# Attention over sorted edges: the softmax weights move to a PSUM bank, and TensorE does the following pair's sums ahead of each step of the chain of maxima

## The chip, the cores and the metric

The kernel runs on one core of one Trainium2 chip. The time is that of one execution on the device in microseconds; the median of several runs counts. The profile is of one execution of its own.

## The reference, cut to what matters

A graph of 6250 nodes and 100,000 edges, sorted by `dst`, goes through two layers. The change is in the first one, an attention along the edges with 8 heads of 32 columns:

```
h = maximum(layernorm(x), 0)
q, k, v = h@Wq+bq, h@Wk+bk, h@Wv+bv          # (6250, 8, 32)
scores = einsum('ehd,ehd->eh', q[src], k[dst]) / sqrt(32)
m = segment_max(scores, dst)
e = exp(scores - m[dst]);  z = segment_sum(e, dst);  p = e / maximum(z[dst], 1e-16)
x = x + segment_sum(v[src] * p[:, :, None], dst)
```

The second layer (a hyperbolic message layer over the same edges) and the last node stage are untouched.

## The kernel before, in words

The kernel has five stages, one after the other: sorting the edges together with the projections, `attention`, `mid_stage`, `messages`, `fin_stage`. The change is inside `attention`.

**Units of work.** 128 edges lie on the 128 partitions and are one step. Two steps are a pair, whose edges all fall into one block of 127 nodes. A turn is 4 pairs (G = 8 steps, SG = 4), a window is 2 turns (16 steps x 8 heads = 128 columns). There are 440 pairs, 110 turns and 55 windows. The code is unrolled over 10 turns and looped.

**One turn `t`,** spread over the engines, each of which has its instructions in a fixed order of its own and waits on semaphores that count:

- SyncE fetches `marks` (which node each edge belongs to), penalties and columns.
- GpSimd issues 8 indirect gathers, one a step, of the rows q|v of `src` into one of 5 ring slots (L1935). A slot is free when VectorE has weighted the rows of the turn five before (`weighed`).
- ScalarE makes the one-hot matrices: `hot_columns` (L2033, L2035) for the products with k, `hot_rows` (L2045, L2048) for the sums.
- TensorE `near` (L1961, tile `kx`): one-hot times the block of k, a pair at a time. VectorE `mult` (L2126) multiplies by q, `score` (L2137) sums over 32 columns into `sc`.
- Three turns later VectorE `weigh` (L2105, two instructions a turn) multiplies the gathered v rows by the softmax weights `pw`, giving `pv`; ScalarE `weight_sums` (L2067) copies the weights beside them.
- Four turns later TensorE `sums` (L1981, tile `out`, two banks in turn) adds the rows of a pair by one-hot matrix, and VectorE `add` (L2147) adds the result into the block's accumulator. So `old` is turn t-4 and `ready` is turn t-3.

**The chain of maxima** runs once a window, in the even turns, and gives each edge the running maximum of its node. It goes back and forth between the two engines, one step for each p = 0..3 of the turn:

- TensorE p = 0: transpose of `sc` into `pT` (L1993, `t1_in`); it waits for `scored`. VectorE `runs_alone` (L2156, L2157, L2159) gives `ended`.
- TensorE p = 1: a small product (L1998, `m1_in`). VectorE `carries` (L2170, L2171) gives `carried`.
- TensorE p = 2: a small product (L2002, `m2_in`). VectorE `maxima` (L2180 to L2194) gives `cleared` and `readied`.
- TensorE p = 3: transpose of `shifted` into `ps` and a small product (L2006, L2008). ScalarE `weights` (L2056) takes exp from `ps` into `pw`, then exp of the block's factor into `fac` (L2059), which VectorE `rescale` (L2115) uses.

VectorE's order in slot p of a turn is `mult`, (`rescale`), `add`, `weigh` (p = 0, 1) or `score` (p = 2, 3), and then its step of the chain (p = 0, 1, 2). TensorE's is

```
sums(old, p)
near(t if p < 2 else t.plus(1), (p + 2) % SG)
if w:
    chain(t, w, p)
```

Of the kernel before, what the change touches and what calls it, by code (L numbers as in the profile page):

```python
# [11 lines left out]
ALU = mybir.AluOpType  # L12
ACT = mybir.ActivationFunctionType
AX = mybir.AxisListType

P = 128
NODES, DIM, HEADS = 6250, 256, 8
DH = DIM // HEADS
# [20 lines left out]
SCORE = 1.0 / math.sqrt(DH)  # L39
G = 8  # L40
# [24 lines left out]
class Stage(ExitStack):  # L65
# [6 lines left out]
    def sem(self, name):  # L72
        handle = self.enter_context(self.nc.semaphore(f"{self.tag}_{name}"))
        self.sems.append(handle)
        return handle
# [1675 lines left out]
SG = G // SPAN  # L1751
WSTEPS = P // HEADS
WG = WSTEPS // G
# [4 lines left out]
BODY = RING * WG  # L1758
# [55 lines left out]
def attention(nc, m, edges):  # L1814
# [17 lines left out]
    with Stage(nc, "at") as ctx:  # L1832
        sb = lambda n, s, d=F32: ctx.enter_context(nc.sbuf_tensor(f"at_{n}", s, d))
        pb = lambda n, s: ctx.enter_context(nc.psum_tensor(f"at_{n}", s, F32))
        sem = ctx.sem
# [7 lines left out]
        hot = sb("hot", [P, 2, G, P])  # L1843
        pv = sb("pv", [P, 2, G, HEADS, HD])
        sc = sb("sc", [P, WSTEPS, HEADS])
        pw = sb("pw", [P, BODY // WG, WSTEPS, HEADS])
        pens = sb("pens", [P, BODY // WG, PEN])
        off = sb("off", [1, SUPER], I16)
        blk = sb("blk", [P, 1 + SUPER])
# [9 lines left out]
        junk = sb("junk", [P, 2, WSTEPS])  # L1859
        kx = pb("kx", [P, 4, 512])  # L1860
        out = pb("out", [P, 2, 512])
        pT = pb("pT", [P, 512])
        ps = pb("ps", [P, 512])
        bc_in = [sem(f"bc_in{h}") for h in range(2)]
        col_in = m.at_col_in
        pen_in = [sem(f"pen_in{h}") for h in range(BODY // WG)]
        got = m.at_got
        (c_in, made, hotT_in, hot_in, z_in, kx_in, mixed, scored, weighed, out_in, summed, t1_in, ran, ended, m1_in, carried, m2_in,
         came_in, topped, cleared, readied, taken, t2_in, m3_in, far_rows, far_cols, p_in, fac_in, rescaled) = (sem(n) for n in (
             "c_in", "made", "hotT_in", "hot_in", "z_in", "kx_in", "mixed", "scored", "weighed", "out_in", "summed", "t1_in", "ran",  # L1870
             "ended", "m1_in", "carried", "m2_in", "came_in", "topped", "cleared", "readied", "taken", "t2_in", "m3_in", "far_rows",
             "far_cols", "p_in", "fac_in", "rescaled"))

        def window_of(t):

# [6 lines left out]
        with nc.Block() as block:  # L1882
# [57 lines left out]
            @block.tensor  # L1940
            def _(pe):
                TE = nc.tensor
                pe.wait_ge(c_in, 32)
                pe.wait_ge(made, 7)
                starts = Starts(pe, "at_pe", off, (NB - 1) * AW, 2)

                def near(t, p):


                    if not t.exists():  # L1950
                        return
                    if p % 2 == 0:
                        starts.fetch(t.n * SG + p, 2)
                    at = starts.values(p % 2, 1)[0]
                    if p == 0:
                        pe.wait_ge(hotT_in, t.n + 1)
                    before = t.plus(-1)
                    if before.exists():
                        pe.wait_ge(mixed, before.n * SG + p + 1)
                    for k in range(SPAN):  # L1960
                        last = TE.matmul(kx[:, p, k * DIM:(k + 1) * DIM], hotT[:, t.h % 2, (SPAN * p + k) * P:(SPAN * p + k + 1) * P],  # L1961
                                         m.keys[:, bass.ds(at, DIM)], start=True, stop=True)
                    last.then_inc(kx_in, 1)

                def sums(t, p):


                    if not t.exists():
                        return
                    if p == 0:  # L1970
                        pe.wait_ge(hot_in, t.n + 1)
                        pe.wait_ge(z_in, t.n + 1)
                    if p % 2 == 0:
                        pe.wait_ge(weighed, 2 * t.n + p // 2 + 1)
                    if p >= 2:
                        pe.wait_ge(summed, t.n * SG + p - 1)
                    elif t.plus(-1).exists():
                        pe.wait_ge(summed, t.plus(-1).n * SG + p + 3)
                    for k in range(SPAN):
                        j = SPAN * p + k  # L1980
                        last = TE.matmul(out[:, p % 2, 0:AW], hot[:, t.h % 2, j, :], pv[:, t.h % 2, j].rearrange("p h d -> p (h d)"),  # L1981
                                         start=(k == 0), stop=(k == SPAN - 1))
                    last.then_inc(out_in, 1)

                def chain(t, w, p):


                    n = w.window
                    if p == 0:
                        pe.wait_ge(scored, 2 * t.n)  # L1990
                        if w.plus(-WG).exists():
                            pe.wait_ge(cleared, n)
                        TE.transpose(pT[:, 0:P], sc.rearrange("p k h -> p (k h)"), m.ident[:, :]).then_inc(t1_in, 1)  # L1993
                    if p == 1:
                        pe.wait_ge(ended, n + 1)
                        if w.plus(-WG).exists():
                            pe.wait_ge(fac_in, n)
                        TE.matmul(ps[0:HEADS, 0:2 * WSTEPS], sel[:, :], ends.rearrange("p v k -> p (v k)"), start=True, stop=True).then_inc(m1_in, 1)  # L1998
                    if p == 2:
                        pe.wait_ge(carried, 2 * n + 2)  # L2000
                        both = carry[:, 0:2 * (WSTEPS + 2)].rearrange("h (v k) -> h v k", v=2)[:, :, 0:WSTEPS]
                        TE.matmul(ps[:, 4 * WSTEPS:6 * WSTEPS].rearrange("p (v k) -> p v k", v=2), selT.rearrange("h k g -> h (k g)"), both,  # L2002
                                  start=True, stop=True).then_inc(m2_in, 1)
                    if p == 3:
                        pe.wait_ge(cleared, n + 1)
                        TE.transpose(ps[:, P:2 * P], shifted[:, :], m.ident[:, :]).then_inc(t2_in, 1)  # L2006
                        pe.wait_ge(readied, 3 * n + 3)
                        TE.matmul(ps[:, 2 * P:2 * P + HEADS], first[:, :], scale[:, :], start=True, stop=True).then_inc(m3_in, 1)  # L2008

                def period(t):  # L2010
                    w = window_of(t)
                    old = t.plus(-LAG - 1)
                    for p in range(SG):
                        sums(old, p)
                        near(t if p < 2 else t.plus(1), (p + 2) % SG)
                        if w:
                            chain(t, w, p)

                near(Turn(0, 0), 0)
                near(Turn(0, 0), 1)  # L2020
                each_turn(pe, period, LAG + 1)

            @block.scalar
            def _(act):
# [25 lines left out]
                def weights(w):  # L2050
                    n = w.window
                    act.wait_ge(m3_in, n + 1)
                    act.wait_ge(t2_in, n + 1)
                    if w.plus(-BODY).exists():
                        act.wait_ge(weighed, 2 * (w.plus(-BODY).n + WG))
                    A.activation(pw[:, w.wslot].rearrange("p k h -> p (k h)"), ps[:, P:2 * P], ACT.Exp, scale=SCORE).then_inc(p_in, 1)  # L2056
                    if w.plus(-WG).exists():
                        act.wait_ge(summed, w.plus(-WG).n * SG + 1)
                    A.activation(fac[:, :], ps[:, 2 * P:2 * P + HEADS], ACT.Exp, scale=SCORE).then_inc(fac_in, 1)  # L2059

                def weight_sums(t):

                    if not t.exists():
                        return
                    act.wait_ge(p_in, t.window + 1)
                    k0 = (t.h % WG) * G
                    A.copy(pv[:, t.h % 2, :, :, DH], pw[:, t.wslot, k0:k0 + G, :]).then_inc(z_in, 1)  # L2067

                def period(t):
                    hot_columns(t.plus(1))  # L2070
# [10 lines left out]
            def _(dve):  # L2081
# [14 lines left out]
                def weigh(t, half):  # L2096
                    if not t.exists():
                        return
                    if half == 0:
                        dve.wait_ge(p_in, t.window + 1)  # L2100
                        if t.plus(-2).exists():
                            dve.wait_ge(out_in, t.plus(-2).n * SG + SG)
                    k = slice(half * (G // 2), (half + 1) * (G // 2))
                    k0 = (t.h % WG) * G + half * (G // 2)
                    V.tensor_tensor(pv[:, t.h % 2, k, :, 0:DH], ring[t.slot][:, k, DIM:2 * DIM].rearrange("p k (h d) -> p k h d", d=DH),  # L2105
                                    pw[:, t.wslot, k0:k0 + G // 2, :].unsqueeze(3).to_broadcast([P, G // 2, HEADS, DH]), ALU.mult).then_inc(weighed, 1)

                def rescale(t, at):

# [689 lines left out]
```

## Time and profile before

| | |
|---|---|
| median of 3 runs | 4433.48 us (4430.65 to 4446.2) |
| the profiled execution, its own time | 4412.6 us |
| its span, first to last instruction | 4410.7 us |
| VectorE busy | 3427.8 us (78%) |
| TensorE busy | 3227.8 us (73%) |
| ScalarE busy | 2222.8 us (50%) |
| GpSimd busy | 1967.7 us (45%) |
| attention stage | from about 742 to 2309 us |

The shares are means over five stages with different limits. The change touches the stage from 742 to 2309 us alone, so that stretch is to be read by itself. A wait that the profile calls `remote` ended with a semaphore update that has no recorded end of an instruction near it; `issue` is a wait that no update explains.

### The profile page before, as it was taken

Reading aid. Unit: us, or ns where it says so; the run is one execution under the profiler, and the core shown is the slowest. Engines: PE = TensorE matmul, PEld = TensorE weight load, DVE = VectorE, ACT = ScalarE, POOL = GpSimd, SP = SyncE. Lnnn points to the kernel's source line nnn. Section 1 sums busy time; section 2 is a strip of 40 time slices with the busy share of each in tenths; the row PEclk is TensorE's granted clock in tenths of the full one; section 3 lists DMA queues with packets and bytes.
Section 4 is the critical chain, followed back from the end, with each engine's and each line's share of the span. In section 5 each row is a group of like instructions: output and inputs, shape, how many; then the busy total and the mean of one; then the engine's idle time right before and its main releaser. Section 6 shows DMA issues by size and latency. Waiting matters only on the chain. (4 is left out here: it accounts for less than half of the span.)

```text
span 4410.7 us, 62580 instructions
## 1 busy us (share of the span) xinstructions
PE 3227.8 (73%) x12662; PEld 2489.5 (56%) x12663; DVE 3427.8 (78%) x9144; ACT 2222.8 (50%) x5988; POOL 1967.7 (45%) x2404
## 2 busy tenths in 40 slices
PE   3656653667767667776674688888888888988786
PEld 2434432545545555555553577777777777777654
DVE  8999995777767777777776377888888887888866
ACT  3245542434434444443446465665665665666556
POOL 1000003556555565555530266666666666666300
PEclk9767665788878888887887899999999999999987
DMA  2111005556666566666636465556555555555351
GB/s 61 36 52 36 20 17 168 172 177 198 187 180 193 179 198 192 188 194 179 194 121 166 139 172 165 157 159 164 157 158 164 161 158 162 162 159 158 89 119 47
DMA packets 295233, 635.08 MB, mean 144 GB/s; under 512 B 78196, under 2 KB 147122, under 8 KB 294656
## 3 DMA queue, kind: packets, MB, share of 16 engines
q0 software_dynamic: 141312, 463.96, 36.9%
q1 hardware_dynamic: 153602, 168.11, 13.7%
q14 instruction: 271, 2.22, 0.2%
q8 instruction: 48, 0.79, 0.1%
HBM read 587.26 MB, written 44.65 MB: 143 GB/s over the span
## 5 line engine op out<-in xcount | busy, mean ns | idle before, releaser
L2372 POOL DMA_INDIRECT area<-d_xr,col x880 | 904.0, 1027 | 733.9 <-DVE area L2609 305.9
L1935 POOL DMA_INDIRECT low<-d_qv,col x516 | 520.3, 1008 | 437.3 <-DVE at_pv L2105 270.8
L2465 PE MATMUL ms_near_a<-low,ms_hotT 128*128 x1760 | 564.7, 404 | 131.8 <-DVE area L2578 83.9
L1981 PE MATMUL at_out<-at_pv,at_hot 128*128 128x264 f32 x1760 | 582.1, 462 | 51.5 <-DVE area L2147 26.6
L1961 PE MATMUL at_kx<-area,tab_c 128*128 x1760 | 537.3, 436 | 31.5 <-issue 25.8
L2466 PE MATMUL ms_near_c<-tab_c,ms_hotT 128*128 x1760 | 554.6, 398 | 0.0
L2465 PEld LDWEIGHTS ms_near_a<-low,ms_hotT 128*128 128x128 f32 x1760 | 342.9, 199 | 215.0 <-issue 164.4
L1935 POOL DMA_INDIRECT tab_c<-d_qv,col x352 | 354.6, 1007 | 231.9 <-DVE at_pv L2105 118.4
L1961 PEld LDWEIGHTS at_kx<-area,tab_c 128*128 128x128 f32 x1760 | 385.9, 223 | 122.9 <-issue 49.0
L1981 PEld LDWEIGHTS at_out<-at_pv,at_hot 128*128 128x128 f32 x1760 | 368.1, 223 | 137.1 <-issue 57.5
L2485 PE MATMUL ms_out<-ms_more,ms_hot 128*128 128x257 f32 x1408 | 381.9, 395 | 74.9 <-DVE ms_hot L2599 63.8
L2507 ACT COPY area<-area 128x2 f32<-128x2 f32 x440 | 82.3, 187 | 632.1 <-DVE area L2578 516.5
L2147 DVE SCALAR_TENSOR_TENSOR area<-area,at_keep,at_out 128x264 f32 x440 | 212.2, 482 | 224.5 <-remote 132.2
L2466 PEld LDWEIGHTS ms_near_c<-tab_c,ms_hotT 128*128 128x128 f32 x1760 | 354.3, 201 | 57.1
L2575 DVE TENSOR_TENSOR ms_more<-area,ms_near_a 128x514 f32<-128x514 f32 x352 | 239.8, 681 | 174.7 <-PE ms_near_c L2468 114.9
L2056 ACT ACTIVATE at_pw<-at_ps 128x128 f32<-128x128 f32 x55 | 15.3, 278 | 669.4 <-PE at_ps L2008 349.5
L2485 PEld LDWEIGHTS ms_out<-ms_more,ms_hot 128*128 128x128 f32 x1408 | 269.5, 195 | 139.7 <-DVE low L2620 43.6
L2609 DVE CUSTOM_DVE_ANT_0 area<-area 128x256 f32<-128x256 f32 x880 | 337.0, 419 | 5.3 <-ACT area L2520 5.3
L2532 ACT ACTIVATE ms_junk<-ms_more 128x255 bf16<-128x255 f32 x704 | 282.2, 402 | 9.9 <-DVE ms_more L2575 0.8
L2599 DVE TENSOR_SCALAR ms_hot<-ramp,col,area 128x128 f32<-128x128 f32 x880 | 265.8, 349 | 11.8 <-issue 10.3
L2468 PE MATMUL ms_near_c<-area,ident 128*128 128x256 f32 x880 | 272.2, 392 | 0.0
L2045 ACT ACTIVATE at_hot<-ramp,col 128x128 f32<-128x128 f32 x880 | 267.5, 386 | 7.0 <-PE at_out L1981 5.2
(360 smaller groups left out, 6677.6 us busy)
## 6 DMA issues: line engine op xcount, KB each, us to landing
tab_c<-by_dst_marks SPq DMA_DIRECT2D x110, 512.0 KB
ms_near_no<-by_src_near SPq DMA_DIRECT2D x110, 224.0 KB
area<-d_xr,col POOLq DMA_INDIRECT x880
d_qv<-low SPq DMA_DIRECT2D x10, 1120.0 KB, 5.0
low<-d_qv,col POOLq DMA_INDIRECT x528
d_xr<-mid_hm SPq DMA_DIRECT2D x5, 1128.8 KB, 5.6
tab_c<-d_qv,col POOLq DMA_INDIRECT x352
first_x<-in_x_dram SPq DMA_DIRECT2D x5, 1120.0 KB
```

What stands on the lines that cost most here:

```text
L1935: pool.indirect_dma_start(out=ring[t.slot][:, k, :], out_offset=None, in_=m.d_qv, in_offset=bass.IndirectOffsetOnAxis(ap=col[:, t.h, k, 0: ...
L1961: last = TE.matmul(kx[:, p, k * DIM:(k + 1) * DIM], hotT[:, t.h % 2, (SPAN * p + k) * P:(SPAN * p + k + 1) * P], m.keys[:, bass.ds(at, DIM ...
L1981: last = TE.matmul(out[:, p % 2, 0:AW], hot[:, t.h % 2, j, :], pv[:, t.h % 2, j].rearrange("p h d -> p (h d)"), start=(k == 0), stop=(k == ...
L2045: A.activation(hot[:, t.h % 2, k, :], m.ramp[:, :], ACT.Abs, scale=-1.0, bias=col[:, t.h, k, 1:2].bitcast(F32)).then_inc(far_rows, 1)
L2372: pool.indirect_dma_start(out=far_rows(t, p)[:, k, :], out_offset=None, in_=m.d_xr, in_offset=bass.IndirectOffsetOnAxis(ap=col[:, t.h, SPA ...
L2465: TE.matmul(near_a[:, (SPAN * p + k) % 4, 0:TW], rows, m.tab_a[:, bass.ds(at, TW)], start=True, stop=True)
L2466: last = TE.matmul(near_c[:, p % 2, k * DIM:(k + 1) * DIM], rows, m.tab_c[:, bass.ds(at, DIM)], start=True, stop=p % 2 == 0)
L2468: last = TE.matmul(near_c[:, p % 2, k * DIM:(k + 1) * DIM], m.ident[:, :], far_rows(t, p)[:, k, XB:XW], start=False, stop=True)
L2485: last = TE.matmul(out[:, p % 2, 0:TW], hot[:, j, :], dd[t.slot][:, j, 0:TW], start=(k == 0), stop=(k == SPAN - 1))
L2532: AC.activation(junk[:, k, 1:DIM], dd[t.slot][:, SPAN * p + k, 1:DIM], ACT.Square, accum_out=SQ[:, t.wslot, at:at + 1]).then_inc(squared, 1)
L2599: V.tensor_scalar(hot[:, k, :], m.ramp[:, :], col[:, t.h, k, 1:2].bitcast(F32), cs[:, t.wslot, at:at + 1], ALU.is_equal, ALU.mult).then_in ...
L2609: V.tensor_tensor_reduce(out=row, in0=row, in1=r_aw2, scale=1.0, scalar=0.0, op0=ALU.mult, op1=ALU.add, accum_out=AL[:, t.wslot, k0 + k:k0 ...
```

## The change

1. `pw`, the weights that `weigh` multiplies by, had 5 window slots in SBUF. Now `weigh` reads them from a PSUM bank of its own, `p_bank`. ScalarE writes them there, and by a second exp of the same `ps` into a single slot `pw` in SBUF, for `weight_sums` alone.
2. To free a bank, `pT` and `ps` share one. So the wait for `fac_in` goes from the chain's step p = 1 to its step p = 0.
3. ScalarE's first exp waits for `weighed` of the window before (it was of five windows before), and what follows it for `z_in` of the window before.
4. TensorE's order: each step of the chain comes after the sums of the following pair. In a turn without a chain the order of products and sums is as it was.

```diff
-        pw = sb("pw", [P, BODY // WG, WSTEPS, HEADS])
+        pw = sb("pw", [P, 1, WSTEPS, HEADS])
-        pT = pb("pT", [P, 512])
-        ps = pb("ps", [P, 512])
+        small = pb("ps", [P, 512])
+        pT, ps = small[:, 0:P], small[:, P:512]
+        p_bank = pb("p", [P, 512])
+        p_rows = p_bank[:, 0:WSTEPS * HEADS].rearrange("p (k h) -> p k h", h=HEADS)
...
                         if w.plus(-WG).exists():
                             pe.wait_ge(cleared, n)
+                            pe.wait_ge(fac_in, n)
                         TE.transpose(pT[:, 0:P], sc.rearrange("p k h -> p (k h)"), m.ident[:, :]).then_inc(t1_in, 1)
                     if p == 1:
                         pe.wait_ge(ended, n + 1)
-                        if w.plus(-WG).exists():
-                            pe.wait_ge(fac_in, n)
...
                     for p in range(SG):
-                        sums(old, p)
                         near(t if p < 2 else t.plus(1), (p + 2) % SG)
+                        sums(old if p + 1 < SG else old.plus(1), (p + 1) % SG)
                         if w:
                             chain(t, w, p)
...
-                    if w.plus(-BODY).exists():
-                        act.wait_ge(weighed, 2 * (w.plus(-BODY).n + WG))
-                    A.activation(pw[:, w.wslot].rearrange("p k h -> p (k h)"), ps[:, P:2 * P], ACT.Exp, scale=SCORE).then_inc(p_in, 1)
+                    if w.plus(-WG).exists():
+                        act.wait_ge(weighed, 2 * w.n)
+                    A.activation(p_bank[:, 0:P], ps[:, P:2 * P], ACT.Exp, scale=SCORE).then_inc(p_in, 1)
                     if w.plus(-WG).exists():
                         act.wait_ge(summed, w.plus(-WG).n * SG + 1)
+                        act.wait_ge(z_in, w.n)
+                    A.activation(pw.rearrange("p v k h -> p v (k h)")[:, 0, :], ps[:, P:2 * P], ACT.Exp, scale=SCORE).then_inc(p_sum_in, 1)
                     A.activation(fac[:, :], ps[:, 2 * P:2 * P + HEADS], ACT.Exp, scale=SCORE).then_inc(fac_in, 1)
...
-                    act.wait_ge(p_in, t.window + 1)
+                    act.wait_ge(p_sum_in, t.window + 1)
...
-                                    pw[:, t.wslot, k0:k0 + G // 2, :].unsqueeze(3).to_broadcast([P, G // 2, HEADS, DH]), ALU.mult).then_inc(weighed, 1)
+                                    p_rows[:, k0:k0 + G // 2, :].unsqueeze(3).to_broadcast([P, G // 2, HEADS, DH]), ALU.mult).then_inc(weighed, 1)
```

## Rows read from the trace of the kernel before

**Rows 1.** Attention, messages: us, busy PE, PEld, DVE, ACT, POOL, clock, DMA share, GB/s.
```profile
742.00:2309.00 1567.00, 1097.47 (x3957) 813.24 (x3956) 1158.51 (x2310) 669.08 (x1429) 869.23 (x862) 0.82 0.62 184
2500.00:4000.00 1500.00, 1301.25 (x5511) 1082.62 (x5512) 1195.52 (x4315) 910.60 (x2928) 970.77 (x1350) 0.94 0.59 162
```

**Rows 2.** VectorE's groups in attention: count, busy us, mean ns, idle us before, releasers.
```profile
L2137 DVE TENSOR_REDUCE at_sc<-tab_c 128x32 f32<-128x1024 f32 x220 | 265.4, 1207 | 0.1
L2147 DVE SCALAR_TENSOR_TENSOR area<-area,at_keep,at_out 128x264 f32 x440 | 212.2, 482 | 224.5 <-remote 132.2 <-PE at_out L1981 67.6 <-issue 18.1
L2126 DVE TENSOR_TENSOR tab_c<-low,at_kx 128x512 f32<-128x512 f32 x264 | 178.3, 675 | 54.0 <-issue 42.7 <-remote 8.1 <-PE at_kx L1961 2.1
L2105 DVE TENSOR_TENSOR at_pv<-low,at_pw 128x1024 f32<-128x1024 f32 x132 | 160.7, 1217 | 0.0
...
L2105 DVE TENSOR_TENSOR at_pv<-tab_c,at_pw 128x1024 f32<-128x1024 f32 x88 | 107.2, 1218 | 0.0
...
L2115 DVE TENSOR_TENSOR area<-area,at_fac 128x264 f32 x55 | 23.6, 429 | 1.2 <-issue 1.2
```

**Rows 3.** TensorE's groups in attention, columns as in rows 2.
```profile
L1981 PE MATMUL at_out<-at_pv,at_hot 128*128 128x264 f32 x1760 | 582.1, 462 | 51.5 <-DVE area L2147 26.6 <-issue 19.6 <-ACT at_hot L2048 4.8
...
L2002 PE MATMUL at_ps<-at_carry,at_selT 8*128 8x32 f32 x110 | 28.2, 341 | 90.5 <-issue 42.6 <-DVE at_carry L2171 35.4 <-DVE at_carry L2170 12.3
...
L2006 PE MATMUL at_ps<-ident,at_shifted 128*128 128x128 f32 x55 | 20.9, 379 | 99.7 <-DVE at_shifted L2190 67.9 <-issue 31.4
L1993 PE MATMUL at_pT<-ident,at_sc 128*128 128x128 f32 x55 | 18.3, 333 | 51.2 <-issue 26.4 <-DVE at_sc L2137 24.7
L1998 PE MATMUL at_ps<-at_ends,at_sel 128*8 128x32 f32 x110 | 13.6, 211 | 163.2 <-DVE at_ends L2159 113.3 <-issue 49.9
```

**Rows 4.** VectorE's waits in attention: us in total, times, longest.
```profile
DVE area L2147 <- remote: 132.2, 50, 5.8
DVE area L2147 <- PE at_out L1981: 67.6, 48, 3.7
DVE at_carry L2170 <- remote: 54.7, 17, 9.6
DVE tab_c L2126 <- issue: 42.7, 19, 7.3
DVE at_runs L2156 <- remote: 35.2, 16, 7.5
DVE at_junk L2180 <- remote: 28.8, 15, 4.6
...
DVE area L2147 <- issue: 18.1, 18, 3.6
```

**Rows 5.** Timeline of one even turn: start us, us, instruction, [idle before, releaser].
```profile
1704.92 1.06 PE L1981 MATMUL at_out<-at_pv,at_hot 128*128 128x264 f32 x4
...
1705.98 1.22 DVE L2105 TENSOR_TENSOR at_pv<-low,at_pw 128x1024 f32<-128x1024 f32 x1
1706.56 1.46 POOL L1935 DMA_INDIRECT tab_c<-d_qv,col  x1 [0.31 <-issue]
...
1708.91 0.42 DVE L2156 TENSOR_TENSOR_SCAN at_runs<-at_pens,at_pT 128x128 f32<-128x128 f32 x1 [1.72 <-remote]
...
1709.92 0.23 PE L1998 MATMUL at_ps<-at_ends,at_sel 128*8 128x32 f32 x2 [3.08 <-DVE at_ends L2159]
...
1714.78 0.49 DVE L2147 SCALAR_TENSOR_TENSOR area<-area,at_keep,at_out 128x264 f32 x1 [4.32 <-remote]
```

**Rows 6.** GpSimd's gathers in attention, columns as in rows 2.
```profile
L1935 POOL DMA_INDIRECT low<-d_qv,col x510 | 514.6, 1009 | 424.3 <-DVE at_pv L2105 270.8 <-issue 153.5
L1935 POOL DMA_INDIRECT tab_c<-d_qv,col x352 | 354.6, 1007 | 231.9 <-DVE at_pv L2105 118.4 <-issue 113.4
```

**Rows 7.** The gathers' line by itself: ns min/median/max.
```profile
L1935 POOL DMA_INDIRECT low<-d_qv,col x516: 942/949/1930, 733.8 to 2240.9; - x172
```

**Rows 8.** ScalarE's exp of the weights, columns as in rows 2.
```profile
L2056 ACT ACTIVATE at_pw<-at_ps 128x128 f32<-128x128 f32 x55 | 15.3, 278 | 669.4 <-PE at_ps L2008 349.5 <-issue 167.7 <-remote 125.3
```

More of the change, by code:

```diff
@@ L1868, in attention @@
         (c_in, made, hotT_in, hot_in, z_in, kx_in, mixed, scored, weighed, out_in, summed, t1_in, ran, ended, m1_in, carried, m2_in,
-         came_in, topped, cleared, readied, taken, t2_in, m3_in, far_rows, far_cols, p_in, fac_in, rescaled) = (sem(n) for n in (
+         came_in, topped, cleared, readied, taken, t2_in, m3_in, far_rows, far_cols, p_in, p_sum_in, fac_in, rescaled) = (sem(n) for n in (
              "c_in", "made", "hotT_in", "hot_in", "z_in", "kx_in", "mixed", "scored", "weighed", "out_in", "summed", "t1_in", "ran",
              "ended", "m1_in", "carried", "m2_in", "came_in", "topped", "cleared", "readied", "taken", "t2_in", "m3_in", "far_rows",
-             "far_cols", "p_in", "fac_in", "rescaled"))
+             "far_cols", "p_in", "p_sum_in", "fac_in", "rescaled"))
         def window_of(t):
@@ L2064, in weight_sums @@
                         return
-                    act.wait_ge(p_in, t.window + 1)
+                    act.wait_ge(p_sum_in, t.window + 1)
                     k0 = (t.h % WG) * G
-                    A.copy(pv[:, t.h % 2, :, :, DH], pw[:, t.wslot, k0:k0 + G, :]).then_inc(z_in, 1)
+                    A.copy(pv[:, t.h % 2, :, :, DH], pw[:, 0, k0:k0 + G, :]).then_inc(z_in, 1)
                 def period(t):
```

## The prediction

> **What bounds the kernel now.** First the busy times by stretch [rows 1]: attention takes 1567 us, in which VectorE is busy 1158.5, TensorE 1097.5, GpSimd 869.2 and ScalarE 669.1 us. No engine is full, while in messages VectorE reaches 1195.5 of 1500. So attention loses time in the handing back and forth, and is 1567/55 = 28.5 us a window, of which VectorE works 1158.5/55 = 21.1.
>
> Then VectorE's groups and its waits [rows 2, 4]. It waits for the sums (L2147) 224.5 us, for the chain's three steps 35.2, 54.7 and some 29 us, 119 together in 48 waits, and 54 us before `mult`, of which 42.7 are `issue` in 19 waits; the loop's own jump is the likely part of those, and nothing in the change touches it. That is what is to be had: about 344 us of waits on TensorE. The reader should see that `weigh` (L2105) never waits (0.0): the weights are there in time.
>
> TensorE's groups [rows 3] show the other side: it stands idle ahead of each step of the chain, 51.2, 163.2, 90.5 and 99.7 us for the four, 404.6 us in 220 steps, or 1.84 us each, and the sums behind that step can't start, since the queue is in order. One sum of a pair takes 582.1/440 = 1.32 us on the mean.
>
> The timeline [rows 5] shows how they meet. The sums of pair 1 ran at 1704.92 and were through by 1705.98 in the records; VectorE's add, which takes them, starts at 1714.78 after 4.32 us of `remote`. The transpose before it was awaited until 1708.91, `remote` too. So TensorE's completions reach VectorE microseconds after the recorded work, in a stretch in which GpSimd issues one gather behind the other. Two thirds of the waits for sums counted by cause (132.2 of 217.9) are of this kind. The trace doesn't say why; it does say that every TensorE result that VectorE needs profits from being asked for early, and that results are handed over in order.
>
> **The change part by part.**
>
> *Order on TensorE.* Four sums a window (220 of 440) go ahead of the chain's step that they stood behind. Their inputs are ready: pair p+1 needs the add of p-1 for its bank, which VectorE does before it does what the step waits for; the sums of the next turn at p = 3 need one-hot rows and weight column from ScalarE, for which TensorE waited 4.8 us in all of attention before [rows 3]. So each such sum starts earlier by the idle time ahead of the step, 1.84 us, and the step itself. The waits for sums are 217.9 us in 116 times, 1.88 us each [rows 4]. Half of them, 109 us, should fall on the moved half. The lead is about as long as the mean wait, the longest waits (5.8 us) are only cut: two thirds, 73 us. Ends: 0, if the handing over stands still until a moment that has nothing to do with when the work was issued, and 109.
>
> Against it: a step of the chain now follows one more sum. Where TensorE was idle before it for longer than 1.32 us, the sum fits in. That holds on the mean for steps 1, 2 and 3 (163.2/55 = 2.97, 1.65 and 1.81 us), not for the transpose of step 0 (0.93). VectorE has a cushion behind each step: mult, rescale, add and weigh before it wants the transpose, 0.68 + 0.43 + 0.48 + 1.22 = 2.8 us [rows 2], and 2.4 us for the two next ones. So in an undisturbed window the delay costs nothing. It costs where the cushion was already gone, in the 48 waits for chain steps: 48 x 1.32 = 63 us at most, 0 at least. I take half, 32, since in about half of them the sum should have got through in the idle time.
>
> *Weights in PSUM.* `weigh` is 220 instructions of 1217 ns. Its price from PSUM isn't in the trace. From SBUF alone a product of 264 columns takes 429 ns (L2115) and one of 1024 takes 1217 (L2105), which gives 686 for 512; `mult`, of 512 with one input from PSUM, takes 675 [rows 2]. So PSUM costs nothing: -11 ns, -2 us in 220. The other bound is L2147 less L2115, both of 264 columns, 482 - 429 = 53 ns, 12 us. I take 0. The Trainium skill (Perfetto Trace Analysis, Optimizing Scalar/DVE Operations) gives VectorE about 60 ns of access overhead on SBUF and about 125 on PSUM; by it the 220 instructions would be 14 us longer, close to the high bound, and the row of `mult` speaks against it.
>
> With both inputs in SBUF `weigh` also meets GpSimd. A gather's instruction takes 949 ns in the median and 942 at least, but 1930 at most and 1009 on the mean [rows 6, 7]; the 1.46 us one lies beside a `weigh` [rows 5]. The excess is 862 x 0.06 = 52 us. The Trainium skill (SBUF — State Buffer, Who interferes with whom) says that a VectorE instruction with two SBUF inputs contends with a GpSimd instruction that reads SBUF; the trace agrees, with that 1.46 us. The 52 us go, but GpSimd stands idle 389.2 us of this stage waiting for `weigh` to free slots [rows 6], and a turn's eight gathers take 8 x (1.01 + 0.30) = 10.5 of 14.2 us. So what it saves becomes more waiting: 0 on the path.
>
> *ScalarE.* A second exp, 55 x 0.28 = 15 us, and `fac` 0.28 us later. It comes behind the one that `weigh` waits for, and ScalarE idles 669.4 us before that exp [rows 8]: 0. If that cover were gone it would be 15 us. The new waits for `weighed` and `z_in` of the window before ask for instructions that VectorE did in slots 0 and 1 of the same turn and ScalarE itself just before, while the exp comes after slot 2: 0. What stands behind them on ScalarE is `fac` and the next one-hot columns.
>
> *The shared bank* puts `fac_in` ahead of the transpose, behind which sums and products queue; `fac` of the window before was made a whole turn earlier, some 14 us: 0.
>
> **Sum.** -73 + 32 = -41 us on the profiled execution's 4412.6, 4371.6. The median of the runs is 4433.48, 1.0047 times as much, so 4392.
>
> **The rivals.**
>
> *The wait only changes its place.* What is not waited for at the add is waited for at the next step of the chain, since both hang on TensorE's late handing over. For it: the chain's waits are `remote` almost entirely [rows 4]; a cause outside the order would stay. Against: 67.6 us of the waits for sums ended with the sums' recorded end, which an earlier start moves. Then gain and cost are 0 to -20 us, in the middle 4402.6, or 4423 as a median.
>
> *Steps of the chain stuck behind the sums: slower.* In the stretches where TensorE hands over late, the sum put ahead delays the step, and VectorE must have the step first. Before, it did its scans and the next `mult` while the sum came; now it can't. If every one of the 48 waits grows by 1.32 us and nothing is gained, it is +63 us: 4412.6 + 63, 4497 as a median. It decides from where more than 73/1.32 = 55 of the 220 steps come a full sum later to a VectorE that is already waiting. For it: in the timeline the transpose came at 1708.91 but the sums behind it only by 1714.78; the other way round the transpose too would have come then, and VectorE would have lost the scans, the ends and a mult, about 1.7 us. With a gain of half the size beside it, about 4460.
>
> *The full gain,* all of the 109 us, perhaps with gathers that end sooner: 4412.6 - 109, 4324.
>
> *Gathers were the bound after all.* Then the port's 52 us come off: 4381. VectorE never waits for gathered rows by name, so this is weak.
>
> **How the numbers follow.** About 0.5% (22 us) is what a measurement of this kernel can tell from no change. The forecast case (-15 to -75) has 0.42, the change of place 0.23, slower 0.20, the full gain 0.12, the port 0.03. Faster by over 0.5%: 0.36 of the forecast case, 0.12, 0.02, in all 0.50. Slower by over 0.5%: 0.20 and 0.01 for weights that cost more from PSUM, 0.21. Within: 0.29. The range goes from 4335, which leaves out the far half of the full gain, to 4465, which takes in the slower case up to its middle. The forecast case alone is 4355 to 4420.
>
> **What would show it.** Right: VectorE's idle time ahead of L2147 falls from 224.5 to about 150 us, TensorE's idle time ahead of L1998, L2002, L2006 shrinks by the sums put there, `weigh` stays within 1205 to 1270 ns, the gathers' mean falls to about 950 ns, and GpSimd's idle time grows. Wrong: waits of the scans (L2156), carries (L2170) and maxima (L2180) that rise from 119 us by more than the adds' fall; a wait of TensorE's sums for ScalarE's one-hot rows in front of step 3; a wait of `weigh` for its weights; or late completions that become rarer or more frequent with the gathers' pace, which nothing in this trace lets me price.

## The result, and the profile after

The changed kernel takes 4515.36 us (median of 4, 4507.35 to 4518.93) against 4436.1 (4 runs): 1.020 times the kernel before, 95% interval 1.016 to 1.024. It is slower by 79 us where 41 us less was forecast. Two more timings, on chips 1 and 12, gave 1.022 (1.014 to 1.030) and 1.023 (1.020 to 1.026).

Nearly all of it is in attention. From the first to the last matmul of `sums` it went from 788.4 to 2308.5 us before and goes from 794.6 to 2401.2 after, 1520 and 1607 us. VectorE does the same work in a longer stage; the columns are those of [rows 1].

```profile
742.00:2409.00 1667.00, 1116.66 (x3960) 812.26 (x3960) 1155.98 (x2314) 679.05 (x1486) 823.26 (x865) 0.80 0.58 174
2600.00:4100.00 1500.00, 1307.67 (x5522) 1085.49 (x5523) 1198.09 (x4324) 911.77 (x2933) 966.35 (x1351) 0.93 0.59 162
```

VectorE's groups in attention after, to be held against [rows 2] (L2150 is the add, L2108 weigh, L2159 the first scan, L2173 carries, L2183 maxima):

```profile
L2150 DVE SCALAR_TENSOR_TENSOR area<-area,at_keep,at_out 128x264 f32 x440 | 211.3, 480 | 58.5 <-issue 32.9 <-remote 10.9 <-PE at_out L1983 9.8
...
L2108 DVE TENSOR_TENSOR at_pv<-low,at_p 128x1024 f32<-128x1024 f32 x132 | 160.1, 1213 | 1.9 <-ACT at_p L2057 1.3 <-issue 0.7
...
L2159 DVE TENSOR_TENSOR_SCAN at_runs<-at_pens,at_ps 128x128 f32<-128x128 f32 x55 | 22.9, 417 | 110.5 <-remote 110.5
...
L2183 DVE CUSTOM_DVE_ANT_0 at_junk<-at_ps,at_pick 128x16 f32<-128x16 f32 x110 | 14.3, 165 | 40.4 <-PE at_ps L2003 13.8 <-remote 13.7 <-issue 12.7
L2173 DVE TENSOR_TENSOR_SCAN at_carry<-at_breaks,at_carry,at_ps 8x16 f32<-8x16 f32 x55 | 12.8, 232 | 223.0 <-remote 215.7 <-issue 7.1
```

The waits for sums fell by 224.5 - 58.5 = 166 us. The waits for the chain rose from 35.2 + 54.7 + 33.7 = 123.6 to 110.5 + 223.0 + 40.4 = 373.9, by 250. The difference is 84 us, close to the loss of 79. Weighing itself costs the same, 1213 ns for 1217.

TensorE and GpSimd, against [rows 3, 6]:

```profile
L1963 PE MATMUL at_kx<-area,tab_c 128*128 x1760 | 566.2, 453 | 102.4 <-issue 53.3 <-DVE tab_c L2129 29.1 <-ACT tab_c L2036 18.9
...
L2003 PE MATMUL at_ps<-at_carry,at_selT 8*128 8x32 f32 x110 | 31.2, 372 | 199.7 <-DVE at_carry L2174 184.5 <-issue 15.2
...
L2007 PE MATMUL at_ps<-ident,at_shifted 128*128 128x128 f32 x55 | 19.9, 362 | 17.1 <-DVE at_shifted L2193 16.8
L1996 PE MATMUL at_ps<-ident,at_sc 128*128 128x128 f32 x55 | 16.5, 300 | 7.9 <-DVE at_sc L2140 7.4 <-issue 0.5
```
```profile
L1937 POOL DMA_INDIRECT low<-d_qv,col x513 | 489.6, 954 | 491.8 <-DVE at_pv L2108 337.3 <-issue 153.4 <-DMA col<-by_dst_edge_cols 1.2
```

The idle time ahead of the transpose went from 51.2 to 7.9 us and ahead of the last transpose from 99.7 to 17.1: the sums fill it, as the change wants. But ahead of the second small product (L2003), which needs `carries`, TensorE now stands idle 199.7 us, where it was 90.5. A gather instruction takes 954 ns on the mean for 1009.

The timeline of one even turn after shows what VectorE waits for:

```profile
1689.63 0.33 PE L1996 MATMUL at_ps<-ident,at_sc 128*128 128x128 f32 x1
...
1693.02 0.19 DVE L2162 TENSOR_TENSOR at_ends<-at_pick,at_runs 128x32 f32<-128x32 f32 x1
...
1693.27 0.23 PE L1999 MATMUL at_ps<-at_ends,at_sel 128*8 128x32 f32 x2 [0.78 <-issue]
...
1694.13 1.21 DVE L2108 TENSOR_TENSOR at_pv<-low,at_p 128x1024 f32<-128x1024 f32 x1
...
1702.96 0.95 POOL L1937 DMA_INDIRECT low<-d_qv,col  x1 [0.30 <-issue]
...
1707.07 0.23 DVE L2173 TENSOR_TENSOR_SCAN at_carry<-at_breaks,at_carry,at_ps 8x16 f32<-8x16 f32 x1 [11.72 <-remote]
...
1707.43 0.63 PE L2003 MATMUL at_ps<-at_carry,at_selT 8*128 8x32 f32 x2 [11.18 <-DVE at_carry L2174]
```

The small product ran at 1693.27, for 0.23 us. `carries`, which needs it and no transfer, starts at 1707.07, after VectorE has stood for 11.72 us; TensorE stood for the last 11.18 of them, and ScalarE longer. The only engine that computed was GpSimd, with one gather after the other until it ran out of free ring slots (1702.96, the last). The reader should see the order: gathers end, their traffic runs out, and at once VectorE is let go. The semaphore updates in the trace for the four TensorE steps that ended from 1692.49 to 1696.26 all fall between 1707.00 and 1707.16. The profile models the ends of matmuls, so it can't tell work that ended late from a signal that came late; "late completion" stands for either below. The stretches of the same turn say it in traffic (last two numbers: DMA share, GB/s):

```profile
1692.50:1707.00 14.50, 2.24 (x10) 1.53 (x10) 2.81 (x6) 0.00 (x0) 8.67 (x10) 0.70 0.77 231
1708.00:1712.00 4.00, 4.00 (x11) 2.73 (x10) 3.90 (x15) 0.00 (x0) 0.00 (x0) 0.50 0.03 4
```

**Was the step itself late?** The sum now ahead of each step can make TensorE begin it later. The starts in the two traces, all 55 windows, say by how much. The transpose starts 0.75 us behind its scores, where it was 0.16. The first small product starts 0.12 us behind `ends` (0.42 at most), where it was 0.10 (0.40). The second starts 1.38 us behind `carries`, where it was 0.58. So the product that `carries` needs was not held up by the sum, and yet the wait for it grew most, by 168 us. It was VectorE that heard of it later. In the windows where `carries` waited over 0.2 us, it started 6.6 us behind the product's recorded end before (17 windows) and 12.5 us after (21).

The ends of these waits differ too. Of the 21 waits of `carries` over 1 us after the change, 20 end more than 1 us behind GpSimd's last gather. Before, 2 of 17 do, and the other 15 end while GpSimd is still in its gathers.

### The profile page after: what moved, and what is told of

Same layout as the page of the kernel before. It is cut to its first block and busy times, and to the rows that moved or that the text cites. A ratio compares the mean times of both kernels' runs of the same rounds, so it can differ in the third digit from the quotient of the medians.

```text
span 4505.6 us, 62645 instructions
## 1 busy us (share of the span) xinstructions
PE 3237.9 (72%) x12662; PEld 2483.3 (55%) x12663; DVE 3422.8 (76%) x9144; ACT 2231.0 (50%) x6043; POOL 1914.9 (43%) x2404
## 5 line engine op out<-in xcount | busy, mean ns | idle before, releaser
L2375 POOL DMA_INDIRECT area<-d_xr,col x880 | 900.8, 1024 | 742.9 <-DVE area L2612 319.0
L1937 POOL DMA_INDIRECT low<-d_qv,col x516 | 492.5, 954 | 501.4 <-DVE at_pv L2108 337.3
L1963 PE MATMUL at_kx<-area,tab_c 128*128 x1760 | 566.2, 453 | 102.4 <-issue 53.3
L1983 PE MATMUL at_out<-at_pv,at_hot 128*128 128x264 f32 x1760 | 561.6, 449 | 96.0 <-DVE area L2150 64.5
L1983 PEld LDWEIGHTS at_out<-at_pv,at_hot 128*128 128x128 f32 x1760 | 379.4, 222 | 214.1 <-issue 93.2
L1963 PEld LDWEIGHTS at_kx<-area,tab_c 128*128 128x128 f32 x1760 | 366.3, 223 | 186.8 <-issue 128.6
L1937 POOL DMA_INDIRECT tab_c<-d_qv,col x352 | 333.9, 949 | 304.3 <-DVE at_pv L2108 198.4
L2057 ACT ACTIVATE at_p<-at_ps 128x128 f32<-128x128 f32 x55 | 14.4, 262 | 870.8 <-PE at_ps L2009 560.3
L2140 DVE TENSOR_REDUCE at_sc<-tab_c 128x32 f32<-128x1024 f32 x220 | 265.2, 1205 | 0.1
```

The costliest lines, as they stand in the source:

```text
L1937: pool.indirect_dma_start(out=ring[t.slot][:, k, :], out_offset=None, in_=m.d_qv, in_offset=bass.IndirectOffsetOnAxis(ap=col[:, t.h, k, 0: ...
L2375: pool.indirect_dma_start(out=far_rows(t, p)[:, k, :], out_offset=None, in_=m.d_xr, in_offset=bass.IndirectOffsetOnAxis(ap=col[:, t.h, SPA ...
```

## The experiments

Theory A: the order does it, a chain step handed over behind one more sum. Theory B: the weights in PSUM do it. Theory C, beneath both: TensorE's completions are held back while gathers follow each other without a gap. The chips are numbered; every ratio is taken between runs on one chip.

**The halves by themselves.** Order alone is the kernel before with this edit:

```diff
-                        sums(old, p)
                         near(t if p < 2 else t.plus(1), (p + 2) % SG)
+                        sums(old if p + 1 < SG else old.plus(1), (p + 1) % SG)
```

The other half is the changed kernel with this edit undone. A third moves the sums ahead of the steps p = 2 and 3 only.

> The kernel before with TensorE's new order alone; the weights stay in SBUF and the two banks apart. Theory A, the order does it (a sum ahead of each chain step delays it where TensorE's completions arrive late): nearly all of the loss, 4435 + 60 to 90 us, so 4495 to 4525, with VectorE's waits for sums (L2147) down from 224 us to 50 to 80 and those for the transpose and the first small product (L2156, L2170) up from 90 to 300 or more. Theory B, the weights in PSUM do it (faster gathers, shared bank): within 15 us of 4435.

> The changed kernel with TensorE's old order: weights in PSUM, shared bank, two exps. Theory A: within 20 us of the kernel before (4415 to 4455), with the mean gather instruction at 950 ns and no longer stage. Theory B: 4495 or more.

> The kernel before with the sums moved ahead of the steps p = 2 and p = 3 of the chain only; ahead of the transpose (p = 0) and of the first small product (p = 1) the old order stays. In the changed kernel the waits for p = 0 and p = 1 rose by 75 and 161 us and that for p = 2 by 7. Theory A with the damage in the first two steps: 4380 to 4435, the waits for the sums of pair 3 and of the next turn's pair 0 gone and those of L2156 and L2170 as before. Rival, any sum ahead of any step hurts, half of the loss: about 4475.

Measured: 3853.3, 3834.69 and 3866.19 us, beside 3847.64 for the kernel before: ratios 1.0022 (1.0006 to 1.0037), 0.9968 (0.9954 to 0.9982) and 1.0051 (1.0033 to 1.0068). The surprise is the kernel before itself, 13% faster than in the result above. These runs lay on chip 7. On it VectorE's waits in attention, with the new order, are (to be held against [rows 4]):

```profile
DVE tab_c L2126 <- issue: 28.4, 8, 4.0
DVE at_junk L2180 <- PE at_ps L2002: 16.1, 20, 1.0
DVE tab_c L2126 <- PE at_kx L1961: 10.1, 6, 3.6
```

No wait there is `remote`, and the add waited 9.1 us in all. So on this chip completions come when the work ends. The waits that the change is about don't exist there, and none of the three versions differs from the kernel before by more than about 0.5%. The theories could not be told apart; the halves were run again.

> TensorE's new order alone, again, for a chip on which completions come late (the kernel before at about 4410 to 4440). There theory A gives 1.5 to 2.5% more than the kernel before, with the waits of L2156 and L2170 at 300 us or more; if the chip has none of the late completions (the kernel before at 3848), within 0.5% as in the first run of it. Theory B: on a late chip too within 0.5%.

> The changed kernel with TensorE's old order, again, for such a chip. Theory A: 0 to 1% faster than the kernel before (on the chip without late completions it was 0.3% faster). Theory B, gathers issued faster make the bursts denser and completions later still: 1.5% or more slower.

On chip 2, with late completions (the kernel before 4423.97), order alone takes 4476.57, 1.0128 (1.0101 to 1.0155), and the weights in PSUM alone 4504.28, 1.0187 (1.0156 to 1.0218). So both halves cost, where A had given nearly all of the loss to the order and B all of it to the weights. The two together (1.020 to 1.023) are less than their sum. Order alone, by VectorE's groups:

```profile
L2147 DVE SCALAR_TENSOR_TENSOR area<-area,at_keep,at_out 128x264 f32 x440 | 211.5, 481 | 37.3 <-issue 18.9 <-PE at_out L1981 8.4 <-remote 4.6
L2156 DVE TENSOR_TENSOR_SCAN at_runs<-at_pens,at_pT 128x128 f32<-128x128 f32 x55 | 23.0, 418 | 104.8 <-remote 91.4 <-issue 13.4
...
L2180 DVE CUSTOM_DVE_ANT_0 at_junk<-at_ps,at_pick 128x16 f32<-128x16 f32 x110 | 14.4, 167 | 71.0 <-remote 49.8 <-PE at_ps L2002 15.7 <-issue 5.4
L2170 DVE TENSOR_TENSOR_SCAN at_carry<-at_breaks,at_carry,at_ps 8x16 f32<-8x16 f32 x55 | 12.8, 232 | 191.6 <-remote 182.3 <-issue 9.3
```

That is the exchange of the whole change, 187 us off the adds and 104.8 + 191.6 + 71.0 - 123.6 = 244 us onto the chain (against [rows 2], which are from another comparison). Here too the first small product starts 0.10 us behind `ends`. The weights in PSUM alone leave the adds at 211.9 us and bring `carries` from 54.7 to 175.6, with no sum moved at all:

```profile
L2150 DVE SCALAR_TENSOR_TENSOR area<-area,at_keep,at_out 128x264 f32 x440 | 212.4, 483 | 211.9 <-remote 133.3 <-issue 38.2 <-PE at_out L1983 34.4
...
L2173 DVE TENSOR_TENSOR_SCAN at_carry<-at_breaks,at_carry,at_ps 8x16 f32<-8x16 f32 x55 | 12.7, 231 | 175.6 <-remote 159.4 <-issue 16.1
```
```profile
L1937 POOL DMA_INDIRECT low<-d_qv,col x512 | 489.5, 956 | 515.5 <-DVE at_pv L2108 364.5 <-issue 148.8 <-DMA col<-by_dst_edge_cols 2.2
```

**A gap in the gathers.** GpSimd waits for the landing of its own last turn:

```diff
                     pool.wait_ge(col_in[t.h], (t.i + 1) * 16)
+                    if t.plus(-1).exists():
+                        pool.wait_ge(got[t.plus(-1).slot], t.plus(-1).turns(RING) * (16 * G))
```

> The changed kernel, where GpSimd waits, before it issues a turn's 8 gathers, until the 8 of the turn before have landed. Theory C, TensorE's completions are held back while gathers are in flight without a gap, and a gap lets them through: the waits of 11 us for L2173 go, VectorE's idle time in attention falls by 100 us or more and the kernel gets faster than 4515 by 60 us or more although gathers are issued less closely (8 x 1.25 + about 3 us a turn against a turn of 14 to 15). Rival, the late completions have nothing to do with the gathers: the same waits, and 4515 or longer, since rows come later.

> The changed kernel with GpSimd waiting for the landing of the gathers of the turn before, again, for such a chip. It took 4189 us where the kernel before took 3848 and had no late completions; there the gathers' own wait was the bound. Theory C, a gap in the gathers lets the completions through: 4190 to 4300 on a late chip too, so faster than the kernel before by 3% or more, with next to no remote waits. Rival: remote waits of 300 us or more stay and it is slower than 4515.

On chip 7, without late completions, 4189.22 against 3847.64, 1.089 (1.086 to 1.092): VectorE waits for rows, 352 us. On chip 2, with them, 4362.96 against 4423.97: 0.9862 (0.9843 to 0.9881), where the changed kernel without the gap is 2% slower. The gain is less than half of the 3% expected, since VectorE now waits 253 us for rows. `carries` doesn't wait at all any more, the scan 1.3 us:

```profile
L2161 DVE TENSOR_TENSOR_SCAN at_runs<-at_pens,at_ps 128x128 f32<-128x128 f32 x55 | 22.8, 414 | 1.3 <-PE at_ps L1998 1.3
...
L2175 DVE TENSOR_TENSOR_SCAN at_carry<-at_breaks,at_carry,at_ps 8x16 f32<-8x16 f32 x55 | 12.6, 229 | 0.0
```
```profile
DVE tab_c L2131 <- DMA low<-d_qv,col: 162.4, 47, 6.6
DVE tab_c L2131 <- DMA tab_c<-d_qv,col: 90.2, 28, 6.1
...
DVE area L2152 <- remote: 22.8, 8, 4.6
```

That speaks for theory C: TensorE's instructions are the same in the same order, only GpSimd pauses, and VectorE's `remote` waits fall from 365 us to 24. One rival is left. A VectorE that waits for rows asks for its results later, and part of the lateness could hide behind that wait; no run here parts the two.

**Half the bytes.**

```diff
-                        pool.indirect_dma_start(out=ring[t.slot][:, k, :], out_offset=None, in_=m.d_qv,
+                        whole = t.static and t.n < RING
+                        pool.indirect_dma_start(out=ring[t.slot][:, k, :] if whole else ring[t.slot][:, k, DIM:2 * DIM], out_offset=None,
+                                                in_=m.d_qv if whole else m.in_x,
```

> The changed kernel, where each gather after the first five turns brings one row of 256 values from another table in place of 512 (so attention's numbers are not the reference's): the same number of gathers and descriptors, half the bytes. Theory C1, completions are held by the bytes in flight: the remote waits in attention fall to under 100 us and the kernel takes 4250 or less on a late chip. Theory C2, they are held while GpSimd issues, whatever the bytes: the remote waits stay above 250 us and the time above 4400.

4515.81 us, one run, and the waits are those of the changed kernel although traffic from 1000 to 2000 us is 108 GB/s for 180:

```profile
L2175 DVE TENSOR_TENSOR_SCAN at_carry<-at_breaks,at_carry,at_ps 8x16 f32<-8x16 f32 x55 | 12.7, 231 | 220.3 <-remote 220.2
```

So it isn't the bytes (C1 falls). Chip 7 says the same from its side: its attention moves 240 GB/s with no late completion. It says more: its gathers follow each other 42 at a time on the mean with the new order alone and 15 with the weights in PSUM alone, a gap being over 1 us of idle GpSimd, against 9 to 10 in the versions without a pause on the chips with late completions. So dense gathers go with late completions only on a chip that has them at all.

**Which part of the PSUM side.** The weights in PSUM with the old order again, but `weigh` reads the SBUF copy:

```diff
-                        dve.wait_ge(p_in, t.window + 1)
+                        dve.wait_ge(p_sum_in, t.window + 1)
...
-                                    p_rows[:, k0:k0 + G // 2, :].unsqueeze(3)...
+                                    pw[:, 0, k0:k0 + G // 2, :].unsqueeze(3)...
```

> As e2b (weights in PSUM with TensorE's old order), but weigh reads the SBUF copy that the second exp makes; shared bank, moved waits and second exp stay. Theory D: what costs on the PSUM side is that weigh no longer stretches GpSimd's gather instructions, whose pauses let TensorE's held completions through. Then on a chip with late completions the mean gather instruction is back at about 1000 ns and the time is back within 0.5% of the kernel before (e2b was 1.9% slower). Rival E, the shared bank, the moved waits or the second exp cost it: still 1.5% or more slower.

4435.91 against 4423.11, 1.0023 (0.9988 to 1.0058): back at the kernel before. The gather instructions are stretched again, and `carries` waits 64.1 us:

```profile
L1937 POOL DMA_INDIRECT low<-d_qv,col x516 | 522.4, 1012 | 419.9 <-DVE at_pv L2108 249.8 <-issue 156.4 <-POOLq L82 12.4
```

The shared bank, the moved waits and the second exp cost nothing that shows within 0.6%; the operand's place costs the 1.9%.

**The gap in the kernel before, every turn and every second turn** (`if t.h % WG == 0 and ...`), and the latter with weights in PSUM and the old order:

> The kernel before, where GpSimd waits for the landing of the gathers of the turn before, and nothing else changed. Theory C, the gap alone removes the held completions: about as e4b, 4340 to 4400 on a late chip, 1 to 2% faster than the kernel before. If e4b's gain needed the new order or the PSUM weights, it is within 0.5% of the kernel before.

> The kernel before, where GpSimd waits so ahead of every second turn only. In e4b VectorE then waited 252 us for gathered rows; with half as many gaps that should be 100 us or less, while completions still get through once a window. Theory C: 4250 to 4350 on a late chip, the fastest so far. Rival, one gap a window leaves bursts of 20 us in which the chain is held: 4400 or more.

> The same gap ahead of every second turn, in the kernel with weights in PSUM and TensorE's old order. Gather instructions are not stretched there, so a turn's gathers are 0.5 us shorter: as e8 or up to 0.5% faster, if the held completions are gone. If theory D holds and one gap a window isn't enough, it is slower than e8.

4562.69, 4404.58 and 4422.27 against 4423.11: 1.0321 (1.0302 to 1.0340), 0.9948 (0.9913 to 0.9984) and 0.9988 (0.9957 to 1.0018). With a gap every turn no `remote` wait is left here either, but VectorE waits for gathered rows, which it never did before:

```profile
DVE tab_c L2128 <- DMA low<-d_qv,col: 301.0, 56, 10.8
DVE tab_c L2128 <- DMA tab_c<-d_qv,col: 197.6, 38, 9.6
```

Its gather instructions take 1080 and 1063 ns on the mean, for 959 and 954 in the changed kernel with the same gap. That is some 100 us in 866 instructions; it doesn't fully explain why VectorE waits for rows 246 us more. I expected 4340 to 4400: wrong. With a gap every second turn the chain is free (18.5 and 3.3 us) and the adds wait more, 312.9 us; the expected 4250 to 4350 was too good, and the late completions have moved to the adds. It is 0.5% faster than the kernel before. Of all versions only this one and the changed kernel with a gap every turn beat it on such a chip. On chip 7 this one wasn't run. The third version, weights in PSUM, is level with the kernel before; the intervals of the last two overlap.

**A pause that doesn't empty the queue, and the late steps again** (the same wait after the second gather of a turn, `if k == 2`):

> The kernel before, where GpSimd waits once a turn for the landing of the 8 gathers of the turn before, but only after it has issued 2 of the next, so the queue is never left empty by it. If TensorE's completions are held by a queue that never empties, this gives no relief: the remote waits stay near 250 us and it is at the kernel before's time or slower. If a short pause of issuing is enough to let them through (as the stretched gather instructions suggest), the remote waits halve without the 500 us of waits for rows of e5, and it is 1 to 3% faster than the kernel before on a late chip.

> The same wait in the kernel with weights in PSUM and TensorE's old order, whose gather instructions aren't stretched. Theory D with a short pause enough: as e11 or up to 1% faster, since its gathers come sooner (e4b, with PSUM weights, waited 252 us for rows, e5 without them 499). If a pause isn't enough: near e2b, 1.5 to 2% slower than the kernel before.

> The kernel before with the sums ahead of the chain's steps p = 2 and p = 3 only, again, for a chip with late completions. If the order's loss sits in the first two steps, where VectorE's waits rose most, it is within 0.5% of the kernel before or faster; if any sum ahead of any step hurts, 0.5 to 1% slower (all four were 1.3% slower).

These lay on chip 7, without late completions: 3956.07, 3899.73 and 3857.85 against 3847.42, ratios 1.0292 (1.0272 to 1.0312), 1.0143 (1.0126 to 1.0159) and 1.0035 (1.0021 to 1.0049). What they were made for stays open. They do show that where VectorE waits for rows, PSUM weights help: 1.4% against 2.9% lost, with gather instructions of 947 against 1117 ns.

**The two kernels again.**

> The changed kernel again, unaltered. In the four runs before this the kernel before took 3848 us, not 4436, and VectorE had no wait that ended as remote in attention. If the loss needs TensorE's late completions (theory C), then on such a chip the changed kernel is at the kernel before's time, within 0.5%: about 3850 us where that takes 3848, and at 4515 only where the kernel before takes 4436. Rival, the loss is in the order or the PSUM weights themselves: 2% slower here too, 3925 us.

> The kernel before, unaltered, for its profile on this chip. Theory C: at 3848 us no remote waits of VectorE in attention and the stage some 350 us shorter or more; at 4436 us some 250 us of them.

> The changed kernel once more, unaltered. On a chip where the kernel before takes 3848 us and no completion is late: within 0.5% of it, 3830 to 3866, as its halves alone were there (order +0.2%, weights in PSUM -0.3%). On one where it takes 4410 to 4440: 1.8 to 2.4% slower. The rival, that the two halves together cost more than each alone whatever the chip: 1% or more slower on the first kind too.

4515.98 against 4408.04 and 4530.27 against 4425.97, on chips 1 and 12, both with late completions; the kernel before's single run was 4423.53, with the waits of [rows 4] (adds `remote` 128.3 us in 50, carries 66.0 in 17). The whole change on chip 7 was never timed.

## Why the prediction was wrong

- **What bounds the kernel: right.** Attention's waits between TensorE and VectorE, most of them late hand-overs; the loss is there alone.
- **The gain of the order: right in kind, too small.** 73 us were taken, 109 at most; the adds' waits fell by 166. Counted by pair in the two traces, the moved half waited 129.6 us and now waits 6.1, where 109 of it were thought to be there and a third to stay. The other half, which was given no gain, fell from 95.0 to 52.4.
- **The cost of the order: this step failed.** "48 x 1.32 = 63 us at most" priced a chain step put behind a sum at that sum's duration, and 32 us were taken. The chain's waits rose by 250 us. The sum in front is not what did it: the first small product starts as promptly as before (0.12 us behind `ends` for 0.10), and the wait for it rose by 168 us, because VectorE heard of it 12.5 us behind its recorded end instead of 6.6. The missing term is how late a completion is where the engine now asks for it. Order alone has the loss without the PSUM weights (53 us), and a pause of GpSimd takes the waits away.
- **The rivals.** I gave "slower" 0.20 and had its sign, but its price was again the sum's 1.32 us in each of the 48 waits; its scene (the transpose at 1708.91, the sums by 1714.78) saw a completion held, and put that at 1.7 us. "The wait only changes its place" had the exchange right, for the reason that both hang on late handing over, but priced it at 0 to -20 us. Its remark that a cause outside the order would stay is what the rows bear out.
- **Why it is worse than an exchange: open.** A wait for a sum was one add, with work of the same window behind it; a chain wait is a round trip, which VectorE answers and TensorE takes up again. In the timeline TensorE sat idle 11.18 us for the answer, and from 1708 to 1712 it was granted 0.50 of its clock (1.2 GHz), where the four products with k take 2.08 us for 1.13 before the wait. A second candidate: in the turn of [rows 5] VectorE stopped at the add, ahead of the second `weigh`, and GpSimd ran out of slots after 12 gathers (1698.83 to 1714.28). After, VectorE gets past that `weigh` (1694.13) and stops at `carries`, and the slots it freed carry the burst to 16 gathers (1683.98 to 1703.91). When a wait of `carries` over 1 us ended, the burst had 9.9 gathers on the mean before and 15.3 after. That is how the rows read; no run tests either.
- **The weights in PSUM: the price of the instruction was right** (1213 ns for 1217) **and the conclusion "0 on the path" failed:** by themselves they cost 80 us. The larger access overhead that the Trainium skill gives for PSUM (Perfetto Trace Analysis, Optimizing Scalar/DVE Operations) doesn't show in this trace. The contention with GpSimd went: a gather takes 954 ns on the mean for 1009, and 1012 again with the operand back in SBUF. The Trainium skill (SBUF — State Buffer, Who interferes with whom) has it so, and the trace agrees. But the unstretched gather was no gift. With the operand in PSUM the kernel loses 1.9%, with it in SBUF 0.2%; nothing else differs but the semaphore that `weigh` waits on.
- **Why unstretched gathers cost: open.** The thought that a stretched instruction is a pause which lets completions through rests on one gather of 1.46 us in [rows 5], and a count over the same trace doesn't bear it out: of the 80 chain and add waits over 1 us that ended amid gathers, 22 had a gather over 1.05 us in the last 3.5 us. With 12% of gathers that long and three in such a stretch, chance gives about as many. The run meant to test it fell on chip 7, where it couldn't.
- **ScalarE, the moved waits, the shared bank: right,** 0 within 0.6% (the run with the operand in SBUF).
- **A slip in reading.** The `remote` waits for sums, 132.2 of 217.9 us, are 61%, not two thirds. No term hangs on it.
- **The forecast's frame.** The median of the kernel before belongs to chips with late completions; on chip 7, at 3848, both halves are within 0.5%. One profile couldn't tell that.

## What to carry to other kernels

Before moving work ahead of a hand-shake between two in-order engines, look at how late the hand-shake's results arrive, not only at how long the moved work takes. Here a wait taken away at the adds came back larger at the chain, though the chain's product started as early as before. Read both ends of a wait: when the awaited work ran, and when the waiting engine went on. If the two lie microseconds apart, moving the work prices nothing.

An engine that is "not the bound" may still set the time through its rhythm. Making GpSimd's gathers shorter cost 1.9%, and a pause for them turned a loss of 2% into a gain of 1.4%. So test such a freed engine by slowing it on purpose. And time a change on more than one chip: on chip 7 neither half of this one cost over 0.5%.

## What the runs showed of the hardware

- In the timings on chips 1, 2 and 12 and in the result's own profiles, TensorE's completions reached VectorE late while gathers from GpSimd's queue were under way: in the timeline 13.6 us behind the recorded end of a product, and together with the whole backlog when the gathers' traffic ended (231 GB/s, then 4). They don't always wait for that end: in the kernel before, 15 of the 17 waits of `carries` over 1 us ended amid gathers. On chip 7, with 240 GB/s in the same stage, none was late, and the same kernel took 3848 us for 4424. Why chips differ is open.
- Fewer bytes didn't help: 108 GB/s gave the same waits (220.3 us) as 180, in one run. With a pause for landings once a turn the `remote` waits were 24 us in the changed kernel and none in the kernel before.
- A VectorE product of 1024 columns whose second input moves from SBUF to PSUM takes the same time, 1217 and 1213 ns, but stretches the gather instructions beside it less (mean 1009 to 954 ns).
